# A delta-rule stage rewritten: one function set for Exp and Ln, squares and gates read from PSUM, four-way products at its end, a norm weight folded into a matrix, and new instruction orders

## The reference

```python
xz = swapaxes(layernorm(x) @ W_in, 1, 2); xc, zc = split(xz, 2, axis=1)
xs = silu(dwconv(xc, conv_x_w, conv_x_b)); zs = silu(dwconv(zc, conv_z_w, conv_z_b))
q, k, v = heads(xs @ W_q), heads(xs @ W_k), heads(xs @ W_v)       # 4 heads, 24 / 24 / 48 wide
gk   = -exp(A_log) * softplus(xs @ W_gk + dt_bias)
beta = sigmoid(xs @ W_b + b_b)
q, k = l2norm(q), l2norm(k)                                       # rsqrt(sum(x*x) + 1e-6)
S = S * exp(g_t); u = b_t * (v_t - k_t S); S = S + k_t u; o_t = q_t S    # over the 64 positions
o = o * rsqrt(mean(o*o) + 1e-5) * g_norm_w * silu(xs @ W_g)
x = x + concat([o @ W_so, zs]) @ W_out
```

## Time and profile before

| what | value |
|---|---|
| median of 3 runs | 2383.33 us (2377.45 to 2383.9) |
| span of the profiled execution | 2313.3 us |
| median less that span (what lies around the instructions) | 70.0 us |
| busy: PE, PEld | 85%, 71% |
| busy: DVE, ACT, POOL | 69%, 54%, 49% |
| mean granted TensorE clock | 0.931 |

### The profile page before, as it was taken

One profiled execution on the slowest core, in us unless ns is written; L12 is line 12 of the kernel. 1 busy time (PEld: TensorE's weight loads), 2 busy tenths in 40 slices (PEclk: granted clock), 3 DMA queues, 4 the chain that ended last, 5 costly groups with the idle time before them and its releaser, 6 DMA issues.

```text
span 2313.3 us, 66487 instructions
## 1 busy us (share of the span) xinstructions
PE 1964.8 (85%) x27020; PEld 1633.0 (71%) x27020; DVE 1603.6 (69%) x4253; ACT 1255.5 (54%) x2880; POOL 1124.5 (49%) x1336
## 2 busy tenths in 40 slices
PE   5899978889788998899999689667588999898982
PEld 3767757677576776777777478667477888697882
DVE  6589786787857888678767835665889666854232
ACT  5457875467654777657765435234344455443551
POOL 2775336742367633675255354351877222234466
PEclk8999989999899999999999789789699999998996
DMA  4000000000000000000010065797011000026994
GB/s 142 5 6 2 2 1 6 6 2 2 1 3 6 3 2 1 5 5 3 2 38 13 8 187 167 222 235 266 25 28 31 4 9 9 4 83 228 349 315 125
DMA packets 98047, 147.35 MB, mean 64 GB/s; under 512 B 32016, under 2 KB 72464, under 8 KB 97488
## 3 DMA queue, kind: packets, MB, share of 16 engines
q1 hardware_dynamic: 88656, 124.48, 17.0%
q0 software_dynamic: 9088, 18.63, 3.3%
HBM read 126.49 MB, written 16.58 MB: 62 GB/s over the span
## 4 chain that ended last, share of the span: by engine, by line
PE 53%; DVE 24%; issue 8%; POOL 8%; ACT 4%; DMA 2%; SPq 0%; POOLq 0%; DVEq 0%; ACTq 0%
PE PS L2108 5%; PE PS L2092 5%; PE PS L1578 3%; PE PS L1584 3%; PE PS L1060 3%; PE PS L674 3%; PE PS L660 2%; POOL GOT L1736 2%; DVE mx L1054 2%; DVE P L1056 2%; PE PS L1067 2%; PE PS L1075 2%; PE PS L1036 2%; DVE zo L636 2%; PE PS L1171 2%
## 5 line engine op out<-in xcount | busy, mean ns | idle before, releaser
L2122 ACT ACTIVATE wh<-PS,we 128x128 f32<-128x128 f32 x624 | 176.0, 373 | 231.5 <-PE PS L2092 231.0
L1990 POOL DMA_INDIRECT wx<-x,INV x156 | 153.1, 981 | 204.5 <-PE PS L2099 106.0
L2092 PE MATMUL PS<-wxT,we 128*128 128x128 f32 x1248 | 176.3, 289 | 42.5 <-issue 35.1
L1054 DVE TENSOR_REDUCE mx<-PS 128x8 f32<-128x512 f32 x256 | 176.1, 688 | 45.8 <-PE PS L1049 24.0
L640 POOL TENSOR_TENSOR xrs<-xrs,Cs 128x2 f32<-128x2 f32 x112 | 82.0, 732 | 255.0 <-DVE xrs L632 252.7
L2108 PE MATMUL PS<-we,wh 128*128 128x128 f32 x1248 | 181.4, 290 | 22.8 <-DVE wxT L2140 21.1
L2092 PEld LDWEIGHTS PS<-wxT,we 128*128 128x128 f32 x1248 | 161.0, 202 | 49.5 <-issue 48.7
L2108 PEld LDWEIGHTS PS<-we,wh 128*128 128x128 f32 x1248 | 163.8, 202 | 32.2 <-DVE wxT L2140 29.3
L1056 DVE TENSOR_TENSOR P<-PS,mx 128x512 f32<-128x512 f32 x256 | 177.1, 692 | 8.9
L1060 PE MATMUL PS<-Cs,P 128*128 128x128 f32 x1024 | 157.5, 287 | 28.1 <-ACT P L1473 21.0
L1500 POOL TENSOR_TENSOR km<-qk,Cs 128x1024 f32<-128x1024 f32 x64 | 121.1, 1898 | 119.8 <-ACT qk L1458 48.1
(11 more groups left out here) (359 smaller groups left out, 5427.2 us busy)
## 6 DMA issues: line engine op xcount, KB each, us to landing
we<-in_wf SPq DMA_DIRECT2D x78, 578.0 KB, 5.6
we<-in_wl SPq DMA_DIRECT2D x78, 578.0 KB, 5.9
yf<-wy SPq DMA_DIRECT2D x78, 64.0 KB, 5.1
ys<-wy SPq DMA_DIRECT2D x78, 64.0 KB, 5.1
x<-X SPq DMA_DIRECT2D x32, 128.0 KB, 1.9
R<-in_wa SPq DMA_DIRECT2D x1, 3072.0 KB, 14.6
wx<-x,INV POOLq DMA_INDIRECT x156, 5.5
X<-in_x SPq DMA_DIRECT2D x4, 512.0 KB, 15.0
```

The lines of the kernel that those rows point to most:

```text
L1054: e.tensor_reduce(A.mx[r], S3, AX, ALU.max).then_inc(*o.inc())
L1990: e.indirect_dma_start(out=WB[s].x[q // NS % NX], out_offset=None, in_=x1[k], in_offset=bass.IndirectOffsetOnAxis(ap=INV[k % NH][:, q - T0 ...
L2092: i = e.matmul(ps(s, 1)[:, 128 * f:128 * f + 128], w[:, 128 * f:128 * f + 128], B.xT, True, True)
L2122: i = e.activation(B.h[:, 128 * f:128 * f + 128], ps(s, 1)[:, 128 * f:128 * f + 128], ACT.Relu, bias=w[:, 512 + f:513 + f])
```

## The change

- **Function sets.** A helper `act_table` states which set the next function needs and loads it when another is loaded. Exp and Ln are taken from one set, `natural_log_exp_and_others`, everywhere. In the order of ACT the kernel before has 91 loads, the changed one 38, all but the last few of either in phase "one".
- **Projections.** q, k and the gate columns come first (200 columns per tile, both tiles into one bank, one copy to `qk`), then g and then v through `pe_gv`: matmuls with 64 weight columns each, whose results go to alternating halves of the partitions, laid out as the block products want them. Silu reads g from PSUM; v is multiplied by beta straight from PSUM on DVE (`d_bv`), with beta rearranged by four small reciprocals (`d_bS`). The square of q and k is ACT Square from PSUM. The Silu of the z half (`d_silu.1`) moves behind these.
- **Masked keys.** `km` is written by one DVE instruction from PSUM (96x1024), `kq` by one ACT copy (96x512).
- **Products at the end.** The five products behind the inversion (all of `pe_blocks` but the one of XT0) go over four quarters of the array: `pe_swapped` and the new `pe_swapped48`.
- **Tail.** ACT squares o from PSUM, DVE multiplies o by the gate from PSUM meanwhile, ACT computes the -1/2 power as Ln and Exp, one DVE multiplication follows. POOL has no part in it. W_so times the first half of W_out is computed once, at the start, in group 3's first steps, scaled by the norm weight, and kept as `wso`; the product by W_so, its copy and the multiplication by `gnw` go.
- **Orders.** All strings in `ORDER`, for both phases, are new; the instructions of phase "last" are the same apart from its function set.

```diff
+        def act_table(e, name):
+            if loaded[0] != name:
+                e.preload_act_table_set(name)
+                loaded[0] = name
+        def pe_swapped48(e, s, left, right):
+            L4, R4 = blocks4(left), right.rearrange("p (x h d) -> p x h d", x=2, h=4)
+            for h in range(4):
+                for r, x in FOUR:
+                    k = slice(64 * r, 64 * r + 64)
+                    i = e.matmul(ps(s, r)[64 * x:64 * x + 64, 48 * h:48 * h + 48], L4[k, x, h, :], R4[k, x, h, :], True, True)
+            return i
+        def pe_gv(e, s, dst, B, w):
+            for b, t in product(range(2), range(NT)):
+                i = e.matmul(dst[64 * t:64 * t + 64, 192 * b:192 * b + 192], B.cv[0][:, 128 * t + 64 * b:128 * t + 64 * b + 64], w, True, True)
+            return i
...
-            pe_blocks(e, ps(s, 1), B.XT, B.bv.rearrange("p t n -> p (t n)"), 48).then_inc(*sig.inc(G, "d_ups", 0))
+            pe_swapped48(e, s, B.XT, B.bv).then_inc(*sig.inc(G, "d_ups", 0))
...
-            e.matmul(psW(s, 0), w_a("wso")[:, 0:128], B.kq[:, 0:W], True, False)
-            e.matmul(psW(s, 0), w_a("wso")[0:64, 128:256], B.kq[0:64, W:2 * W], False, True).then_inc(*sig.inc(G, "d_so"))
-            yield
-            e.wait_ge(*sig.at(G, "d_yF"))
+            e.wait_ge(*sig.at(G, "d_oF"))
             for t in range(NT):
                 o = ps(s, 1)[:, 128 * t:128 * t + 128]
-                e.matmul(o, B.cv[0][:, 128 * t:128 * t + 128], w_a("wout")[:, 0:128], True, False)
-                i = e.matmul(o, B.cv[1][:, 128 * t:128 * t + 128], w_a("wout")[:, 128:256], False, True)
+                e.matmul(o, B.cv[1][:, 128 * t:128 * t + 128], w_a("wout")[:, 128:256], True, False)
+                e.matmul(o, B.kq[:, 128 * t:128 * t + 128], wso[:, 0:128], False, False)
+                i = e.matmul(o, B.kq[0:64, W + 128 * t:W + 128 * t + 128], wso[0:64, 128:256], False, True)
...
-            e.activation(B.g4, B.g4, ACT.Ln, bias=1.0).then_inc(*sig.inc(G, "d_ex"))
-            e.activation(B.rn, B.rn, ACT.Ln).then_inc(*o.inc())
+            e.activation(B.rn, B.rn, ACT.Ln, bias=c("eps6")).then_inc(*o.inc())
             e.wait_ge(*o.now())
             e.activation(B.rn, B.rn, ACT.Exp, scale=-0.5).then_inc(*sig.inc(G, "d_rn"))
...
-            e.activation(B.o, v3(ps(s, 0)[:, 0:NT * 192], NT), ACT.Copy).then_inc(*sig.inc(G, "d_o"))
+            e.activation(v3(B.km[:, 0:192 * NT], NT), ps48(s), ACT.Square).then_inc(*sig.inc(G, "d_osq"))
+            act_table(e, "natural_log_exp_and_others")
+            e.wait_ge(*sig.at(G, "d_osum"))
+            e.activation(rn, rn, ACT.Ln, bias=c("eps5"), scale=1.0 / 48).then_inc(*o.inc())
+            e.wait_ge(*o.now())
+            e.activation(rn, rn, ACT.Exp, scale=-0.5).then_inc(*sig.inc(G, "d_orn"))
...
+            e.tensor_tensor(B.o, ps48(s), v3(B.sg, 2), ALU.mult).then_inc(*sig.inc(G, "d_og"))
...
-            e.tensor_tensor(o16, o16, bc(rw("gnw"), 1, 4 * NT), ALU.mult).then_inc(*o.inc())
-            e.wait_ge(*o.now())
-            e.wait_ge(*sig.at(G, "d_sg"))
-            e.tensor_tensor(B.o, B.o, B.vg[:, :, 192:384], ALU.mult).then_inc(*sig.inc(G, "d_on"))
+            e.tensor_tensor(o16, o16, bc(rn, 2, 48), ALU.mult).then_inc(*sig.inc(G, "d_on"))
```

More of the change, by code:

```diff
@@ L45 @@
     ("ident", 128), ("sl", 128), ("unit", 64), ("le", 64), ("nm0", 64), ("nm1", 64), ("nm2", 64), ("nm3", 64), ("nm4", 64), ("nn", 64),
-    ("later", 64), ("causal", 64), ("m64", 2), ("parity", 2), ("m8", 8), ("m24", 4), ("tri", 64), ("half", 1), ("before", 128), ("ones", 128), ("iota", 128), ("part", 1), ("back", 8),
+    ("later", 64), ("causal", 64), ("m64", 2), ("parity", 2), ("m8", 8), ("m24", 4), ("tri", 64), ("half", 1), ("before", 128), ("ones", 128), ("iota", 128), ("part", 1), ("back", 8), ("eps6", 1), ("eps5", 1),
 ])
@@ L51 @@
     ("a2_xg", 1), ("a2_xb", 1), ("a2_yg", 1), ("a2_yb", 1), ("a2_3g", 1), ("a2_3b", 1), ("a2_li2b", 4),
-    ("ipb", 2), ("vb", 1),
+    ("ipb", 2), ("vb", 1), ("gnw", 2),
 ])
@@ L716, in pe_delta @@
             yield
-            e.wait_ge(*sig.at(G, "d_et"))
+            e.wait_ge(*sig.at(G, "d_bv"))
+            e.wait_ge(*sig.at(G, "d_kn"))
+            for t in range(NT):
+                i = e.transpose(ps(s, 1)[0:96, 128 * t:128 * t + 128], B.qk[:, t, 104:200], ID)
+            i.then_inc(*sig.inc(G, "d_kT"))
+            yield
+            e.wait_ge(*sig.at(G, "d_et"))
+            e.wait_ge(*sig.at(G, "d_kb"))
+            for t, (a, off) in product(range(NT), ((1, 8), (0, 200))):
+                i = e.transpose(ps(s, 0)[0:96, 256 * t + 128 * a:256 * t + 128 * a + 128], B.qk[:, t, off:off + 96], ID)
+            i.then_inc(*sig.inc(G, "d_kqT"))
+            yield
+            kqv = B.kq.rearrange("p (t a s) -> p t a s", t=NT, a=2)
+            kmv = B.km.rearrange("p (t h s) -> p t h s", t=NT, h=4)
+            e.wait_ge(*sig.at(G, "d_kq"))
+            e.wait_ge(*sig.at(G, "d_km"))
             for t, h, b in product(range(NT), range(4), range(2)):
@@ L775, in act_delta @@
             e.wait_ge(*sig.at(G, "turn", "d"))
+            if G == NS - 1:
+                e.wait_ge(*l_vec.done())
+                e.activation(wso[:, 0:128], ps(s, 1)[:, 0:128], ACT.Copy, scale=cl("gnw", 0))
+                e.activation(wso[0:64, 128:256], ps(s, 1)[0:64, 128:256], ACT.Copy, scale=cl("gnw", 1)[0:64])
             e.activation(B.xF, psW(s, 0), ACT.Copy).then_inc(*sig.inc(G, "colF", "d"))
@@ L807, in act_delta @@
             yield
[L808 to L818 removed]
+            act_table(e, "natural_log_exp_and_others")
             e.wait_ge(*sig.at(G, "d_dt"))
             e.activation(B.ET, ps(s, 0), ACT.Exp).then_inc(*sig.inc(G, "d_et"))
+            yield
+            e.wait_ge(*sig.at(G, "d_kqT"))
+            e.activation(B.kq[0:96], ps(s, 0)[0:96], ACT.Copy).then_inc(*sig.inc(G, "d_kq"))
             yield
@@ L826, in act_delta @@
             e.wait_ge(*sig.at(G, "d_xtT"))
-            e.activation(B.XT, ps(s, 0), ACT.Copy).then_inc(*sig.inc(G, "d_xtA"))
+            e.activation(v3(B.XT, 2), PSt[:, 2 * s:2 * s + 2, 0:256], ACT.Copy).then_inc(*sig.inc(G, "d_xtA"))
             yield
@@ L912, in dve_delta @@
             e.tensor_tensor(v3(B.PP, n8), bc(c("le"), 1, n8), bc(B.g4.rearrange("p t h -> p (t h)"), 2, 64), ALU.mult).then_inc(*sig.inc(G, "d_gr"))
+            yield
+            for t, b in product(range(NT), range(2)):
+                i = e.reciprocal(B.bes[64 * t:64 * t + 64, b, :], B.be1[64 * b:64 * b + 64, t, :])
+            i.then_inc(*sig.inc(G, "d_bS"))
+            e.wait_ge(*sig.at(G, "d_bS"))
+            e.wait_ge(*sig.at(G, "d_vp"))
+            e.tensor_tensor(B.bv.rearrange("p (a d) -> p a d", d=48), ps(s, 1)[:, 0:NT * 192].rearrange("p (a d) -> p a d", d=48),
+                            bc(B.bes.rearrange("p b h -> p (b h)"), 2, 48), ALU.mult).then_inc(*sig.inc(G, "d_bv"))
+            yield
+            kmv = B.km.rearrange("p (t h s) -> p t h s", t=NT, h=4)
+            e.wait_ge(*sig.at(G, "d_kT"))
+            e.tensor_tensor(kmv[0:96], bc(v3(psW(s, 1), NT)[0:96], 2, 4), bc(bc(c("m24")[0:96], 1, NT), 3, 128), ALU.mult).then_inc(*sig.inc(G, "d_km"))
             yield
@@ L2409 @@
     wa = {"win": I[A + "W_in"],
-          "wtm": _np.concatenate([I[A + n] for n in ("W_v", "W_g", "W_gk", "W_b", "W_q", "W_k")], axis=1),
-          "wso": _np.concatenate([I[A + "W_so"][:128], rows(I[A + "W_so"][128:])], axis=1),
+          "wtm": _np.concatenate([I[A + n] for n in ("W_gk", "W_b", "W_q", "W_k", "W_g", "W_v")], axis=1),
+          "wsoT": I[A + "W_so"].T,
           "wout": split(I[A + "W_out"], 2)}
@@ L2425 @@
         col[pf + "_li2b"] = I[k + "li2_b"].reshape(4, 128).T
+    g4 = _np.tile(I[A + "g_norm_w"], 4)[:, None]
+    col["gnw"] = _np.concatenate([g4[:128], rows(g4[128:])], axis=1)
     col["vb"] = I[Fn + "in_proj_b"][256:, None]
@@ L2430 @@
            "outb": Fn + "out_b", "f1g": Fn + "ln1_g", "f1b": Fn + "ln1_b", "f2g": Fn + "ln2_g", "f2b": Fn + "ln2_b",
[L2431 removed]
+           "bout": "L1_attn_b_out", "alog": A + "A_log", "gateb": Fn + "gate_b"}
     row = {k: I[v] for k, v in row.items()}
```

353 lines of the change are left out of this document (154 added, 199 removed), and 26 rows, old and new, of the table STEPS.

## The result

The changed kernel takes 2449.51 us (2446.75 to 2451.79, 4 runs) against 2381.97 of the kernel before in the same measurement: ratio 1.0274 [1.0246, 1.0303], 67 us slower where 60 us faster was forecast, outside the range. The level of a kernel differs between the chips of the measurements by up to 3% (the kernel before took 2309 to 2382 us), so each ratio is taken on one chip; the profiled execution of before (span 2313.3) and its three timed runs were of different levels. A run's own time is only about 2 us above its span (2446.75 and 2444.9 here), so the "70.0 around it" of the working was a difference of level.

A forecast was written before the change was run, and what follows sets the result against it. Phase one was taken as bound by PE throughput mixed with each group's chain through ACT, DVE and POOL. PE's 45 plus 15 for chains, phase last 0, gave -60: 2383.3 to 2323 us, forecast 2300 to 2350, 8-in-10 range 2290 to 2362.

The forecast's parts named there:

- Phase last has the same instructions in another sequence ... I cost it at 0, with 12 us to either side: Phase last: PE's marks stand almost where they stood, so the new sequence costs 0, within 12 us (1% of 1128).
- The prediction's own last sentence: Sign of error: phase last differing by over 12 us, its new sequence then deciding more than the rewritten stage.
- PE work alone, with idle time as it is: -45: Phase one: PE loses 45.1 us of work, and the time falls by as much if idle time stays.
- (a): PE, five products behind the inversion: from two quarters of the array to four, 92.0 to 59.0 us, saving 33.0.
- the rival: Five products get no faster, 48-column matmuls being limited by issue or weight loads; the 33 us stay, 2356 us; chance 0.13.
- (b): PE, tail: the product by W_so goes, one more 128-column product comes at about 12.4 us; saves 10.0.
- (c): PE, projections: 46.8 us replaced by 17.2 (200 columns) and 27.5 (g and v); saves 2.1.
- The tail of group 0 near 8 us instead of 13.5: Expected sign in the profile after: group 0, from the copy of o to the addition to X, near 8 us.
- the 5 that I took: Tail of each group: its chain through ACT, DVE and POOL gets about 5 us shorter.
- I take the 45 and about a third of what is left ... -60: Whole kernel: PE's 45 us plus 15 for shorter chains, out of an outer bound of -77, gives -60.
- the 40: Phase one, chain alone: 10 us shorter per group, four groups per slot one after another, 40 us.
- Slower: Groups in step lose neighbours' work under waits at starts of rounds 2 to 4; slower from 38 us idle each; chance 0.10.

The follow-up runs named there:

- the run with the products alone: The kernel before, in its own orders, with only its five products behind the inversion over four quarters of the array: ratio 0.9991 [0.9964, 1.0019].
- the spread strings: Changed kernel with old orders of phase last and new phase-one strings that run a round's groups apart and overlap rounds more: ratio 0.9949 [0.9923, 0.9975].
- the strings sorted by the step times of before: Changed kernel with old orders of phase last, phase-one steps placed where the kernel before's trace has them: ratio 1.0246 [1.0205, 1.0287].

## Why the prediction was wrong

**The step that failed: "Phase last has the same instructions in another sequence ... I cost it at 0, with 12 us to either side".** It costs 1.7%, 35 to 39 us: over half of the 67 us lost, and some 0.3 of the 127 us between forecast and result. I compared PE's marks, counts of matmuls ahead of a tile; what the traces show late is the routing's index, by 40 us, and behind it the stream of weights, and PE's marks don't show these. The prediction's own last sentence names this as what would make it wrong. Which engine's string does it stays open: no run exchanges one alone.

**The step that failed in phase one: "PE work alone, with idle time as it is: -45".** The work fell by 31, and the idle time wasn't as it is: it rose by 64. "Issue" rose by some 48 (61.7 against 14.0 us in runs on one chip), the waits for ACT at L723 and L1042 by 22, while those for DVE at the transposes fell by 26. PE's work isn't what phase one follows: the four-way products took 25, 21 and 15 us off it in three orders, and phase one got shorter by 0, 13 and 5. By the terms:
- (a) Five products at 12 us: right as a price, 11.9 (a fifth of L680's 59.4) + 12.6 + 12.5 + 12.2 + 11.3 = 60.5, saved 31.5 of the 33.0. But a price from a group's busy time holds only while PE is supplied and doesn't wait for others. I had the column for the first in front of me: the earlier trace rows has 4.5 us of "issue" beside the 47.2, and the rival named "issue" as the limit, only for the wrong reason (48 columns; the busy time did fall, as priced). That rival's outcome, the 33 us stay, is what the run with the products alone measured in time.
- (b) Mis-sized: without W_so but with one more product, W_out costs 18.5 + 18.2 + 14.8 = 51.5 us. In the earlier trace rows L761, L762 and L768 make 34.8, and L767, counted there as unchanged, was 13.5. So +3 instead of -10. I priced the third product at 12.4; each of the three now costs 231 to 289 ns a row where it was 194 to 211.
- (c) 32.2 + 17.4 = 49.6 against 46.8: +3 instead of -2.

The terms make some -25; the other 5 or 6 us lie in groups that the sum didn't name, L706's transposes (19.6, now 9.8 + 6.7) and the key products (36.0, now 32.8).

**"The tail of group 0 near 8 us instead of 13.5"** failed as well: from 98.66 to 118.33, start to start as in the 13.5, it is 19.7 us. Its instructions are fewer, but each stands in a queue behind the other groups', which are now at the same point: the transposes start at 113.39, 4.8 us after their input is there. With the spread strings the same instructions of the first group to finish take 8.0 us, from 93.4 to 101.4, so the 8 was right for the instructions and wrong for their order. Over the 16 groups the time from the last product to the addition to X fell from 16.9 to 13.3 us in the mean, 3.6 of the 5 that I took.

**"I take the 45 and about a third of what is left ... -60".** From the start of a round to its last delta step it did get shorter, 121 us over four rounds, more than the 40, but in part by the strings and not by the chains: with the spread strings these stretches are 136, 169, 200 and 204 us. What I left out is that the same strings overlap the rounds less and let the cross stage run longer. (Besides, 15 is nearer to half of the 32 left than to a third.) The 60 of the forecast are reached in no run: the best order on record gives the kernel 0.5%, some 12 us.

**The rival "Slower"** named what the changed kernel shows, groups in step and less of a neighbour's work under their waits, but its threshold was wrong: "from 38 us of idle time in each". In the windows above PE idles 23.5, 25.7 and 21.9 at the start of rounds 2 to 4 against 18.9, 22.2 and 12.8. The loss lies over the whole round, so a threshold on its first hundred microseconds could not see it. It got 0.10.

**What was right:** 38 loads, ACT at 684 (forecast 700), products at 12, the masked keys at 1.21 us. DVE was called level and fell by 54 us, which bought nothing either.

**What stays open:** how phase one's 33 us divide between the supply of rows, the overlap of rounds and the waits for ACT. That the strings cause them is shown, since other strings with the same instructions end 47 us earlier. But the spread strings removed supply waits and raised the overlap together, and the strings sorted by the step times of before had few supply waits and the old overlap, and lost more to other waits. No run changes one of the three alone.

## What to carry to other kernels

In a kernel whose engines follow written orders, price an order like a stage: compare when each round or stream can start, on every queue, and measure new code under the old order and old code under the new one before crediting either. Count PE's rows per microsecond beside its busy time, and take a saving of busy time as an upper bound: here 25, 21 and 15 us of it gave 0, 13 and 5. A rewritten stage may need its own order to pay: here, with phase last as before, it was +1.7% in one and -0.5% in another.

## What the runs showed of the hardware

In a stretch of nothing but 64x64 float32 blocks PE's instruction rows came at 256 in 3.45 us at best, 13.5 ns a row, with 1.38 us of idle time whenever such a block of rows was worked off in 2.08. With two quarters of the array in use 64-column blocks take 30 ns a MATMUL row, against the 27 of this limit, so the step to four quarters meets it at once. "TensorEngine Tiling (Array Packing)" of the Trainium skill, section "Theoretical Speedup", allows up to twofold for each dimension of 64; the trace gives 31.4 ns for four quarters and 30.6 for two, in a stretch of nothing else.

30 set loads less, 38 us of ACT work, changed the time by a ratio of 1.0005 [0.9985, 1.0026]: on an engine at 54% of the span their time wasn't on the path.
